# A decoder kernel with the gated decay attention reordered and the cross attention stepped, its scores split in three

## The chip, the cores and the metric

One Trainium2 chip, one core, one launch. The time is the device time of that core in microseconds (us). Profiles are of one execution each. Engines: TensorE (PE, its weight loads PEld), VectorE (DVE), ScalarE (ACT), GpSimd (POOL) and SyncE (SP), which starts the DMAs.

## The reference

A two-layer decoder with layer norm after every part, on x of 2 x 256 tokens of 512 features and a context of 2 x 512 tokens. Each part adds to x, and x is then normalised:

1. causal attention, 32 heads of 128 with 8 key heads, rotary embedding, some keys scaled by 1.5 or 0.5
2. a cross product of x and the context, both rounded to 8 bits
3. a mixing of four streams with a Sinkhorn normalisation of 50 rounds
4. gated decay attention ("l1" in the kernel): queries and keys with rotary embedding, products weighted by exp of summed decays, times values; each head's result is divided by its root mean square, multiplied by the gate, and projected out
5. cross attention ("x"): queries from x, keys and values from the context, both queries and keys divided by their root mean square, softmax over 512 keys, values, projection
6. a 512 x 512 linear map with LoRA parts

Parts 4 and 5 are what the change rewrites.

```
att = softmax(rms(q) . rms(k) / sqrt(128) + mask) @ v      # part 5, per head
x   = layernorm(x + att @ Wo)
y   = ((q . k) * exp(g_i - g_j) * dt_j) @ v                # part 4, per head, j <= i
z   = rms(y) * silu(gate)
x   = layernorm(x + z @ Wo)
```

## The kernel before

Each engine has its own instruction list, written by hand in Python; the order of the list is the order of execution, and semaphores (`wait_ge`, `then_inc`) join the lists. All of x stays in SBUF as four tiles of 128 tokens by 512. The 32 heads are worked in eight groups of four that share a key head; a loop body handles one group g, with buffers alternating by p = g % 2. `piped_groups` writes out the first two and last two groups and loops over the rest.

**Split products.** A matmul of fp32 operands is made of two parts: a high part rounded to fp32r and the rest, low = x - high. `product` (L175 to L181) issues three matmuls: high x high (L179), low x high (L180), high x low (L181). `project_split` does a projection of one head for all 512 tokens, `out_split` one output tile: 12 matmuls of 128 x 512 each, a block in what follows. Attention scores, values and transposes are plain fp32 matmuls, two records each in the profile.

**Decay attention** (`l1_tensor` and the functions beside it). TensorE, for one group: key projection into bank 0, values (32 short records, L1161), four queries, gates 0 and 1, scores(0) of the first sequence (3 matmuls, L1121), gates 2 and 3, outputs(0) (decay times value, L1134 and L1137), scores(1), transposes of z 0 and 1 (`turn_z`, L1145), output tile 0, outputs(1), output tile 1, transposes 2 and 3, output tiles 2 and 3. ScalarE copies projections for the rotary embedding (L148 to L150), takes exponentials and squares, and casts weights to their high part (L966). GpSimd does the sine product (L157), the low part of weights, the gate products and the power -1/2. VectorE does the rotary sum (L163, L167), the decay exponents (L1325), clamps gates (`clamp`), weights scores, makes z (`gated`, L1361), takes the low part of z (`rest`, L1369) and adds tiles to x (L215). All z tiles are transposed in bank 2, one behind the other: `turn_z` of tile n waits for the low part of tile n - 1.

**Cross attention** (`x_tensor` and the functions beside it). A group has eight steps, one for each head and sequence, head outermost. Step s: scores (two matmuls of 128 x 512, L1573, to banks 3 and 4), scale and mask into `logit` (L1814), maximum (L1818), exponentials on ScalarE (L1688), normalise on VectorE (L1826), transposes of probabilities (L1584), their copy (L1697), values (L1596), and the attention as high part (ScalarE, L1706) and low part (VectorE, L1835). TensorE runs scores(s), turn_probs(s-2), values(s-3). VectorE runs logits(s) ahead of normalise(s-1). The four queries of the next group are projected in between, two in the first steps and two in the last; key transposes and all four output tiles come behind the last step. GpSimd makes both parts of wq and wo (`split`: L187 high, L191 low).

**First attention** (`l0_tensor`). It has the form that the cross attention gets: in each of eight steps TensorE issues scores(s), turn_probs(s-1), one block, values(s-1), the block being a query or an output tile of the group before, this one or the next.

SyncE's list starts each weight load once the buffer's reader of the group before has signalled; `l1_wq`, `l1_wg` and `l1_wo` have one buffer each, the cross attention's have two.

## Time and profile before

| | us |
|---|---|
| median of 3 runs | 1659.37 (1658.19 to 1660.63) |
| the profiled execution | 1658.7 |
| its span, first to last instruction | 1656.7 |
| TensorE busy | 1484.6 (90%) |
| VectorE busy | 1075.8 (65%) |
| ScalarE busy | 788.2 (48%) |
| GpSimd busy | 659.9 (40%) |

The execution runs through its stages in order: the first attention up to about 375, cross product, mixing and the context's keys and values up to about 541, the decay attention up to about 1062, the cross attention up to about 1613, the linear map to the end. "Busy" of TensorE counts modelled ends that overlap, so it overstates how much of it is used at its peak; start-to-start distances tell what it really takes. PEclk is the clock granted to TensorE as a share of its full 2.4 GHz.

### The profile page before, as it was taken

How to read it: one execution, taken by the hardware profiler on the slowest of the kernel's cores; microseconds unless marked ns; L12 is line 12 of the kernel's file. 1: busy time of each engine (PE TensorE's matmuls, PEld its weight loads, DVE VectorE, ACT ScalarE, POOL GpSimd, SP SyncE). 2: the span in 40 equal slices, each digit the busy share in tenths (PEclk: the TensorE clock that was granted, in tenths of full speed). 3: DMA queues.
4: the chain of work that ended last, by engine and by line, in shares of the span. 5: the costliest groups of instructions: out<-in, count | busy, mean ns of one | idle time of the engine just before them, and what ended most of it. 6: DMA issues, size and time to landing. Idle time of an engine off the chain costs nothing.

```text
span 1656.7 us, 23145 instructions
## 1 busy us (share of the span) xinstructions
PE 1484.6 (90%) x7186; PEld 1161.1 (70%) x7186; DVE 1075.8 (65%) x2399; ACT 788.2 (48%) x2014; POOL 659.9 (40%) x671
## 2 busy tenths in 40 slices
PE   6999999987999589889889889789898898999996
PEld 5778888774988367767767767567676686776672
DVE  4696776876788676566566566545847648457462
ACT  4655666551222355555465465344545336345340
POOL 4544554420222346446456445363515415333200
PEclk9999999999999699999999999789999999999998
DMA  7011111003132222212212211410120210201000
GB/s 285 1 64 64 64 63 63 30 1 139 42 113 100 96 72 90 89 51 90 89 51 89 89 51 36 155 39 14 64 76 1 76 40 37 76 13 56 1 1 25
DMA packets 30120, 107.56 MB, mean 65 GB/s; under 512 B 3847, under 2 KB 13191, under 8 KB 22104
## 3 DMA queue, kind: packets, MB, share of 16 engines
q1 hardware_dynamic: 30040, 106.58, 17.7%
q8 instruction: 39, 0.64, 0.2%
q14 instruction: 41, 0.34, 0.1%
HBM read 97.07 MB, written 9.50 MB: 64 GB/s over the span
## 4 chain that ended last, share of the span: by engine, by line
PE 49%; issue 20%; DVE 19%; ACT 5%; POOL 5%; DMA 1%; POOLq 0%; DVEq 0%; ACTq 0%; SPq 0%
PE bank L179 9%; PE bank L180 8%; PE bank L181 8%; PE bank L1596 4%; PE bank L1573 3%; DVE logit L1814 2%; PE bank L1584 2%; DVE prob L1826 2%; POOL tmp L157 2%; PE bank L1134 2%; PE bank L278 1%; DVE tmp L1792 1%; PE bank L309 1%; PE bank L1121 1%; PE bank L1542 1%
## 5 line engine op out<-in xcount | busy, mean ns | idle before, releaser
L157 POOL TENSOR_TENSOR tmp<-tmp,sin 128x512 f32<-128x512 f32 x80 | 121.3, 1517 | 209.3 <-ACT tmp L150 208.9
L1688 ACT ACTIVATE prob<-logit,rmax 128x512 f32<-128x512 f32 x128 | 91.3, 715 | 153.8 <-DVE rmax L1818 153.8
L181 PE MATMUL bank<-wo_low,att_high 128*128 128x512 f32 x384 | 155.4, 405 | 0.0
L1573 PE MATMUL bank<-kT,qT 128*128 128x512 f32 x256 | 123.6, 606 | 10.6 <-DVE logit L1814 9.5
L179 PE MATMUL bank<-l_wo_high,att_high 128*128 128x512 f32 x256 | 111.6, 436 | 10.6 <-DVE att_low L558 10.6
L1596 PE MATMUL bank<-probT,v 128*128 128x256 f32 x512 | 121.1, 379 | 0.0
L1814 DVE SCALAR_TENSOR_TENSOR logit<-bank,qss,amask 128x512 f32<-128x512 f32 x128 | 92.4, 743 | 34.5 <-PE bank L1573 25.1
L1457 PE MATMUL bank<-kT,wg 128*128 128x256 f32 x512 | 110.9, 379 | 0.7 <-ACT prob L1475 0.7
L1457 PEld LDWEIGHTS bank<-kT,wg 128*128 128x128 f32 x512 | 97.1, 190 | 14.2 <-ACT prob L1475 1.1
L215 DVE TENSOR_TENSOR x<-x,bank 128x512 f32<-128x512 f32 x96 | 64.8, 683 | 64.3 <-PE bank L181 63.6
L180 PE MATMUL bank<-l_wo_high,att_low 128*128 128x512 f32 x256 | 105.3, 411 | 0.0
L180 PE MATMUL bank<-xT_high,wq_low 128*128 128x512 f32 x256 | 103.4, 404 | 0.0
L163 DVE TENSOR_TENSOR tmp<-tmp,cos 128x512 f32<-128x512 f32 x80 | 75.5, 944 | 41.9 <-ACT tmp L150 41.9
L1596 PEld LDWEIGHTS bank<-probT,v 128*128 128x128 f32 x512 | 92.8, 190 | 10.6
L1584 PEld LDWEIGHTS bank<-ident,prob 128*128 128x128 f32 x512 | 57.7, 140 | 57.2 <-DVE prob L1826 46.0
L1750 POOL TENSOR_TENSOR qss<-qss,half 128x4 f32<-128x4 f32 x32 | 33.8, 1064 | 143.9 <-DVE qss L1797 143.9
L148 ACT ACTIVATE tmp<-bank 128x512 f32<-128x512 f32 x80 | 47.4, 593 | 90.0 <-PE bank L181 83.3
L1697 ACT ACTIVATE probT<-bank 128x512 f32<-128x512 f32 x128 | 69.6, 598 | 42.6 <-PE bank L1584 42.3
L181 PEld LDWEIGHTS bank<-wo_low,att_high 128*128 128x128 f32 x384 | 75.4, 196 | 18.2
L1584 PE MATMUL bank<-ident,prob 128*128 128x128 f32 x512 | 67.7, 275 | 22.5 <-DVE prob L1826 22.3
L167 DVE TENSOR_TENSOR qT<-tmp 128x512 f32<-128x512 f32 x64 | 62.1, 970 | 32.7 <-POOL tmp L157 31.4
L1826 DVE TENSOR_SCALAR prob<-prob,rsum 128x512 f32<-128x512 f32 x128 | 81.5, 678 | 2.3
(254 smaller groups left out, 4017.3 us busy)
## 6 DMA issues: line engine op xcount, KB each, us to landing
wq<-in_l_wq SPq DMA_DIRECT2D x16, 1024.0 KB, 5.9
wo<-in_l_wo SPq DMA_DIRECT2D x16, 1024.0 KB, 4.8
wkv<-in_l_wkv SPq DMA_DIRECT2D x16, 512.0 KB, 5.6
wg<-in_l_wg SPq DMA_DIRECT2D x8, 1024.0 KB, 4.7
wq<-in_x_wq SPq DMA_DIRECT2D x8, 1024.0 KB, 7.0
wo<-in_x_wo SPq DMA_DIRECT2D x8, 1024.0 KB, 4.8
kT<-in_x_wkv SPq DMA_DIRECT2D x8, 512.0 KB, 4.1
kv_keys<-logit SPq DMA_DIRECT2D x8, 512.0 KB, 4.6
```

The source lines that it names most:

```text
L157: eng.tensor_tensor(halves(tmp[4 + j % 2]), halves(tmp[2 + j % 2]), per_batch(sin), ALU.mult).then_inc(sem(f"{l}_sinp"), 1)
L163: eng.tensor_tensor(halves(tmp[j % 2]), halves(tmp[j % 2]), per_batch(cos), ALU.mult).then_inc(sem(f"{l}_cosp"), 1)
L179: eng.matmul(dst, a_high, b_high, start=start, stop=False)
L180: eng.matmul(dst, a_low, b_high, start=False, stop=False)
L181: return eng.matmul(dst, a_high, b_low, start=False, stop=stop)
L1457: last = pe.matmul(bank[KV_BANKS[n % 2]][:, i * 256:(i + 1) * 256], wg[t // CT][:, c, t % CT * P:(t % CT + 1) * P], weights[:, c, :], star ...
L1573: pe.matmul(bank[3 + c][:, :], qT[p][:, h, b * L + c * P:b * L + (c + 1) * P], kT[p][:, b * C:(b + 1) * C], start=True, stop=True)\
L1584: last = pe.transpose(bank[5 + half_][:, kt * L + c * P:kt * L + (c + 1) * P], prob[s % 2][:, c, (2 * half_ + kt) * P:(2 * half_ + kt + 1) ...
L1596: last = pe.matmul(bank[VALUE_BANKS[s % 2]][:, 0:L], v[p][:, b * CT + kt, :], probT[s % 2][:, kt, :], start=(kt == 0), stop=(kt == CT - 1))
L1688: last = act.activation(prob[s % 2][:, c, :], logit[s % 2][:, c, :], ACT.Exp, bias=rmax[s % 2][:, c:c + 1], accum_out=rsum[s % 2][:, c:c + 1])
L1814: dve.scalar_tensor_tensor(logit[s % 2][:, c, :], bank[3 + c][:, :], qss[p][:, 1, h, 2 * b + c:2 * b + c + 1], amask[:, c, :], ALU.mult, A ...
L1826: last = dve.tensor_scalar(prob[s % 2][:, c, :], prob[s % 2][:, c, :], rsum[s % 2][:, 2 + c:3 + c], None, ALU.mult)
```

## The change

Decay attention: `l1_scalar`, `l1_gpsimd`, `l1_vector` are reordered to match a new order of TensorE. Its body is now (the order before is told above):

```
+                query(0)
+                query(1)
+                if isinstance(g, int) and g == 0:
+                    dt_turn(pe)
+                query(2)
+                query(3)
+                gates(0)
+                gates(1)
                 scores(0)
                 gates(2)
+                outputs(0, 0)
+                outputs(0, 1)
+                scores(1)
                 gates(3)
+                if not last_group:
+                    key(n)
+                    value(n, 1 - p, (0, 1))
+                outputs(1, 0)
                 turn_z(0)
+                outputs(1, 1)
                 turn_z(1)
                 out_tile(0)
                 out_tile(1)
                 turn_z(2)
                 turn_z(3)
+                if not last_group:
+                    value(n, 1 - p, (2, 3))
                 out_tile(2)
                 out_tile(3)
```

n is g + 1. The next group's key goes to bank 0 once `gates(3)` has been clamped; its values go to bank 1. z tiles are transposed to banks 2 and 5 by turns; output tiles go to banks 3, 4, 0 and 6 (before 1, 0, 3, 4). VectorE's order behind the ropes is now:

```
                 clamp(0)
                 clamp(1)
                 weights(0)
                 clamp(2)
-                clamp(3)
                 low_weights(...)                           # wo
+                weights(1)
                 mean(0)
+                clamp(3)
+                gated(0)
                 mean(1)
-                gated(0)
                 gated(1)
                 rest(0)
-                weights(1)
+                mean(2)
                 rest(1)
-                mean(2)
+                rope_sum(dve, "l1", n, 0, kT[1 - p][:, 0:T])
+                gated(2)
                 mean(3)
-                gated(2)
                 gated(3)
                 rest(2)
                 rest(3)
```

ScalarE takes both `decays` ahead of the sigmoids, the casts of wo and wq between sigmoids 0, 1 and 2, and squares(2) ahead of headed(1); GpSimd makes wq's low part and two powers ahead of gates 2 and 3. For the first group, ScalarE copies the key and the value ahead of the transposed decay columns (`cols`, which waits for `dt_turn`).

Cross attention: steps run sequence outermost, and TensorE's body is

```
+                for s in range(STEPS):
+                    scores(s)
+                    if s or not first:
+                        turn_probs(s - 1)
+                    if s < 2:
+                        query(g, p, s + 2, ...)
+                    elif s < 4:
+                        if not first:
+                            out_late(s)                    # tiles 2, 3 of group g - 1
+                    elif s < 6:
+                        if not last_group:
+                            query(n, 1 - p, s - 4, ...)
+                    else:
+                        out_early(s - 6)                   # tiles 0, 1 of group g
+                        if not last_group:
+                            turn_keys(n, 1 - p, s - 6, ...)
+                    if s in (1, 2):
+                        query_sums(g, s + 1)
+                    if s in (5, 6) and not last_group:
+                        query_sums(n, s - 5)
+                    if s or not first:
+                        values(s - 1)
```

with split scores in place of one fp32 matmul per bank, for which queries and keys get low parts on VectorE:

```
-                        pe.matmul(bank[3 + c][:, :], qT[...], kT[...], start=True, stop=True)
+                        product(pe, bank[3 + c][:, :], (q_high[p][:, h, rows_], q_low[p][h][:, rows_]),
+                                (k_high[p][:, keys_], k_low[p][:, keys_]), True, True)
+            def keys_rest(m, p, half_):
+                dve.scalar_tensor_tensor(k_low[p][at], bank[5 + half_][:, :], dvec[:, 3:4],
+                                         k_high[p][at].bitcast(F32), ALU.mult, ALU.subtract)
+            def query_rest(m, p, h):
+                dve.tensor_tensor(q_low[p][h][:, :], bank[h % 2][:, :], q_high[p][:, h, :].bitcast(F32),
+                                  ALU.subtract)
```

VectorE's step is, with each condition and its call on one line,

```
+                for s in range(STEPS):
+                    logits(s)
+                    if s >= 2 or not first: low(s - 2)
+                    if s == 0 and not first: add(g - 1, 1)
+                    if s in (1, 2): query_rest(g, p, s + 1)
+                    if s in (3, 4) and not first: add(g - 1, s - 1)
+                    if s == 4 and not last_group: x_key_mean(dve, n)
+                    if s in (5, 6) and not last_group: query_rest(n, 1 - p, s - 5)
+                    if s == 7 and not last_group: add(g, 0)
+                    normalise(s)
+                    if s in (1, 2): query_mean(g, p, s + 1)
+                    if s in (5, 6) and not last_group: query_mean(n, 1 - p, s - 5)
+                    if s == 5 and not last_group: norm_keys(n, 1 - p)
+                    if s in (6, 7) and not last_group: keys_rest(n, 1 - p, s - 6)
```

ScalarE's step is turned(s-1), exps(s), then weight casts (steps 4 and 5: wo in 3 + 1 chunks; 6 and 7: wq of group g + 2, two chunks each), a query (steps 0, 1, 4, 5), squares of the next keys (2, 3), keys_out (6, 7), headed(s-1). GpSimd only takes the low parts of the weights, chunk by chunk, and the powers. In the last group all four adds and the statistics of the layer norm come behind low(7). The squares, mean and power of the first keys move ahead of the layer norm between the stages, and the mask is loaded ahead of the keys. In the first attention only a semaphore is renamed. One buffer (`klow0`, 128 x 1024) is added.

## Rows read from the trace of the kernel before

**Rows 1.** Windows: from:to, length, busy of PE PEld DVE ACT POOL, PEclk, DMA share, GB/s
```profile
135.00:260.00 125.00, 121.53 (x690) 103.10 (x688) 86.01 (x196) 79.21 (x202) 60.08 (x61) 1.00 0.16 64
729.50:790.90 61.40, 54.59 (x266) 43.10 (x265) 38.40 (x89) 33.73 (x83) 32.60 (x30) 0.97 0.23 78
790.90:852.20 61.30, 54.53 (x265) 43.00 (x265) 38.05 (x88) 33.68 (x83) 33.05 (x30) 0.97 0.22 77
795.90:803.00 7.10, 5.44 (x20) 4.32 (x21) 5.53 (x18) 1.38 (x2) 0.00 (x0) 0.76 0.01 3
1262.80:1329.70 66.90, 62.46 (x299) 46.81 (x297) 41.78 (x68) 30.84 (x82) 25.14 (x21) 1.00 0.13 48
1329.70:1396.60 66.90, 62.46 (x299) 46.81 (x297) 41.80 (x68) 30.84 (x82) 25.14 (x21) 1.00 0.13 48
```

**Rows 2.** Waits of TensorE in one decay group: total us, times, longest
```profile
PE bank L1145 <- DVE att_low L1369: 3.1, 2, 1.6
PE bank L1145 <- issue: 2.5, 1, 2.5
```

**Rows 3.** Waits of TensorE in one cross attention group
```profile
PE bank L1584 <- DVE prob L1826: 2.9, 2, 1.7
```

**Rows 4.** Timeline of TensorE in a decay group: start, duration, records
```profile
798.59 0.66 PE L179 MATMUL bank<-l_wo_high,att_high 128*128 128x512 f32 x1
...
799.91 0.63 PE L179 MATMUL bank<-l_wo_high,att_high 128*128 128x512 f32 x1
...
849.33 1.28 PE L1134 MATMUL bank<-v,probT 128*128 128x128 f32 x10
850.45 0.39 PE L1137 MATMUL bank<-v,tmp 128*128 128x128 f32 x2
```

**Rows 5.** Timeline of TensorE in a cross attention group
```profile
1193.59 1.88 PE L1573 MATMUL bank<-kT,qT 128*128 128x512 f32 x4
1195.30 1.04 PE L1584 MATMUL bank<-ident,prob 128*128 128x128 f32 x8
1196.18 1.89 PE L1596 MATMUL bank<-probT,v 128*128 128x256 f32 x8
1197.90 1.88 PE L1573 MATMUL bank<-kT,qT 128*128 128x512 f32 x4
...
1202.46 0.40 PE L180 MATMUL bank<-xT_high,wq_low 128*128 128x512 f32 x1
1202.69 0.40 PE L181 MATMUL bank<-xT_low,wq_high 128*128 128x512 f32 x1
```

**Rows 6.** Groups by line: busy us, mean ns, idle before
```profile
L1814 DVE SCALAR_TENSOR_TENSOR logit<-bank,qss,amask 128x512 f32<-128x512 f32 x128 | 92.4, 743 | 34.5 <-PE bank L1573 25.1 <-ACT prob L1688 7.7
...
L1818 DVE TENSOR_REDUCE rmax<-logit 128x2 f32<-128x1024 f32 x64 | 78.1, 1220 | 2.2
...
L1688 ACT ACTIVATE prob<-logit,rmax 128x512 f32<-128x512 f32 x128 | 91.3, 715 | 153.8 <-DVE rmax L1818 153.8
...
L966 ACT ACTIVATE l_wo_high<-wo 128x512 fp32r<-128x512 f32 x32 | 17.6, 620 | 0.2
```

**Rows 7.** The normalise line alone: ns min/median/max
```profile
L1826 DVE TENSOR_SCALAR prob<-prob,rsum x128: 473/487/1494, 1104.7 to 1595.9; 128x512 f32<-128x512 f32 x128
```

**Rows 8.** Timeline where the two stages begin and end
```profile
594.19 2.74 PE L1121 MATMUL bank<-qT,kT 128*128 128x512 f32 x6
...
1062.26 0.69 DVE L215 TENSOR_TENSOR x<-x,bank 128x512 f32<-128x512 f32 x1 [1.03 <-PE bank L181]
...
1071.60 0.80 PE L179 MATMUL bank<-xT_high,wq_high 128*128 128x512 f32 x1 [1.41 <-DVE xT_low L661]
...
1093.23 3.75 PE L1573 MATMUL bank<-kT,qT 128*128 128x512 f32 x4 [1.01 <-ACT kT L1673]
...
1613.08 0.69 DVE L215 TENSOR_TENSOR x<-x,bank 128x512 f32<-128x512 f32 x1 [1.50 <-PE bank L181]
```

**Rows 9.** Timeline of VectorE: the gated products of two tiles
```profile
807.15 2.34 DVE L1361 SCALAR_TENSOR_TENSOR q<-bank,yss,q 128x128 f32<-128x128 f32 x8
```

More of the change, by code:

```diff
@@ L1729, in x_scalar @@
+                if last_group:
+                    turned(7)
+                    headed(7)
             query(0, 0, 0)
-            squares(0, 0)
-            for h in range(1, GH):
-                query(0, 0, h)
-            keys_out(0, 0)
+            query(0, 0, 1)
+            for half_ in range(2):
+                keys_out(0, 0, half_)
             piped_groups(nc.scalar, body)
@@ L1852, in body, with add @@
[L1852 to L1864 removed]
+                def add(m, t):
+                    residual_add(dve, "x", m, t, bank[t % 2])
```

716 lines of the change are left out of this document (392 added, 324 removed).

## The prediction

> **What bounds the kernel now.** The windows come first: in the two attention stages that the change rewrites, TensorE is the busiest engine by far, 54.5 of 61.3 us of a group of the gated decay stage and 62.5 of 66.9 us of a group of the cross attention, with VectorE second (38 and 42 us) [rows 1]. Both stages repeat a group eight times with a fixed period: neighbouring stretches of 61.4 and 61.3 us of the decay stage hold the same work (266 and 265 matmul records), and so do two of 66.9 us of the cross attention (299 each), so these are the periods [rows 1]. The waits of TensorE come next. In the decay stage it waits 5.6 us of a group in front of the transposes of z (L1145), the longest 2.5 us [rows 2]; in the cross stage 2.9 us in front of the transposes of the probabilities, the longest 1.7 [rows 3]. So the price of both is mostly TensorE's own work plus some ends of a dependent chain. A third thing shows in the clock: between 795.9 and 803.0 the granted clock is 0.76 [rows 1], right behind the longest wait, and there the products of two heads start 1.32 us apart (798.59 to 799.91) [rows 4], where three matmuls at full clock take 0.70 (below).
>
> **Floors by counting TensorE's work.** Start-to-start times are used, since modelled ends overlap. A split product streams one matmul each 0.2325 us (1202.46 to 1202.69 [rows 5]), so a block of 12 is 2.79 us. An fp32 matmul of 512 columns is two records 0.43 us apart: four records of L1573 go from 1193.59 to 1195.30, 1.72 us [rows 5].
> Decay stage, one group: 13 blocks of 12 (key, 4 queries, 4 gates, 4 outputs) 36.3; 12 score records at 0.43, 5.2; 96 short records (32 of the values, 48 of decay times value, 16 transposes) at 0.112 (ten in 1.12 us, 849.33 to 850.45 [rows 4]), 10.8. Sum 52.3 us, against 61.3.
> Cross stage, one group: 8 blocks of 12, 22.3; scores 8 x 1.72 = 13.8; transposes of probabilities 8 x 0.88 = 7.0 (1195.30 to 1196.18); values 8 x 1.72 = 13.8 (1196.18 to 1197.90); 32 short records of the sums of squares and 8 key transposes at 0.11, 4.4 [rows 4, 5]. Sum 61.3 us, against 66.9.
> The first attention already has the stepped form that the cross attention gets, and in a stretch of it TensorE is busy 121.5 of 125.0 us at clock 1.00 [rows 1]: the form can be run with 3% lost.
>
> **Cross attention, scores.** Each score product goes from one fp32 matmul to three split ones: 6 x 0.2325 = 1.40 in place of 1.72 us a step, 2.6 us less a group. That is only TensorE. VectorE gets four query remainders and two key remainders a group, all 128x512 from a bank, nearest to L1814 at 0.74 [rows 6]: 4.4 us, bringing it from 41.8 to 46 of 60. ScalarE gets eight casts of weights, 0.62 us each (L966 [rows 6]), 5 us, on its 30.8 [rows 1]; GpSimd loses as many. Neither is near its limit. A split stream that starts behind short transposes loses a further 0.1 us, an estimate, some five times more often than before: 0.5 us. Floor of the new group: 61.3 - 2.6 + 0.5 = 59.2.
> Is the step chain covered? VectorE now does normalise(s) ahead of logits(s+1), so its chain is serial: logits and maximum 2 x 0.70 + 1.22, two exponentials 2 x 0.72 with an accumulator read, 1.6, normalise 2 x 0.49 [rows 7] with its reciprocal, 1.1, and hops of 0.2: 5.5 us a step [rows 6]. A TensorE step is scores 1.4, transposes 0.9, a block 2.8, values 1.7, in some sums 0.8: 6.8 to 8.1, mean 7.4. The chain is covered by 1.3 us or more. Where it is thin: step 5 puts the key norms behind normalise (1.3 to 3.4 us), and keys must be turned, cast and subtracted by ScalarE and VectorE in step 6, before the first half of the next transposes; by my count it arrives 0.2 us early. I take 0.8 us of waits a group, 60.0. The bounds are 59.2 (none) and 63.5 (step 5 to 7 all late).
> The normalise row shows what can eat the cover: median 487 ns, but up to 1494 [rows 7], the long ones where GpSimd runs a split; at the long end a normalise adds 2 us and uses the cover up. The Trainium skill (GPSIMD Engine Reference, 8. Key points) has a rule for it: GpSimd contends with VectorE instructions that have two SBUF inputs or run in a 2-port mode. By that rule the remainders read from a bank are free of it, and the six rope sums and gated products of a decay group are not; no row here prices the difference.
> Ends of the stage: the first group starts its scores 10.5 us after the first query instead of 21.6 (1093.23 less 1071.60 [rows 8]), because two queries are left to steps 0 and 1: 4.6 for the first query at the slow clock, 2.8, key transposes 0.9, two casts 1.4, a remainder 0.7. Steps of the first group: 4.2 (nothing to turn), 9.9 (the transposes wait 2.2 for the first normalise), 4.8 and 4.4 (no output block of a group before), 7.6, 7.6, 8.1, 7.2: 54 us. Groups 1 to 6 take 6 x 60. The last group has no next queries in steps 4 and 5, which the chain binds (5 and 6), and ends with output tiles 2 and 3 (9.5): 6.8 + 7.6 + 7.6 + 6.8 + 5 + 6 + 6.5 + 6.8 + 9.5 = 62.6. Sum 10.5 + 54 + 360 + 62.6 = 487. Before, from 1071.60 to the last residual add at 1613.08: 541.5. Gain 54.4 us. Against it, at the end four adds and four statistics now stand behind the last remainder on VectorE, +1.6 us; and a key mean on VectorE and its power on GpSimd (about 1.6 us) stand in front of the layer norm between the stages, +1.2 us. Net 51.6.
>
> **Decay stage.** Nothing is computed differently; the key and value of group g+1 move among the gates and outputs of g, outputs and z alternate, banks are spread. TensorE's 52.3 us stand. The count from the end of gates(3): the next key uses the same bank, so it waits for clamp(3), 0.9 us. VectorE goes on with gated(0), 1.1 (half of the eight products of L1361 [rows 9]), GpSimd's power 1.0, gated(1) 1.1: 4.9 us after gates(3). Then it waits for the headed copies of tiles 0 and 1, which follow TensorE's transposes (rests until 10.9), makes the key's rope sum (12.4), gated(2) (13.5), power, and gated(3): z(3) is ready at 15.9. TensorE has by then done the key 2.8, values 1.8, outputs 2.7, two transposes 0.9, two output tiles 5.6 and one transpose 0.4 behind its wait of 0.9: 15.1, so 0.8 us of wait. In front of scores(0) the last rope sum is done 15.8 us into the group and TensorE arrives at 16.7. So 54 us if all goes as counted; I add 1 us for VectorE slowed by GpSimd: 55, bounds 52.3 and 58. The slow-clock stretch goes with the long wait.
> Entry costs: query(0) now needs the value bank copied out by ScalarE, which comes behind the decay setup; and the transposed columns are copied only after query(1). In times of the trace: value copied by 574.6, query(0) 4.6 at the slow clock, query(1) 2.8, columns copied by 583.4, two queries' copies 3.6, then queries (2) and (3) and two gates to 596.2, where scores(0) start; now they start at 594.19 [rows 8]. In a settled group they start 16.7 us in, so the first starts in effect at 579.5. The last group lacks the next key and value, 6.3 us. End: 579.5 + 8 x 55 - 6.3 = 1013.2 against 1062.0, just ahead of the last residual add at 1062.26 [rows 8]. Gain 48.8 us.
> The earlier mask load and the weight loads (1 MB in 5 to 7 us) lie beside work; the semaphore rename in the first attention costs nothing.
>
> **Sum.** 48.8 + 51.6 = 100.4; the profiled span 1656.7 becomes 1556.3, and its own time 1658.7 becomes 1558.3. That execution lies 0.7 us under the median of the runs, so 1559.
>
> **Rivals.**
> (a) All waits go: 52.3 and 59.2 a group. Decay gains 8 x 2.7 = 22 more, cross 6: 1531. For it, the first attention's 3%; against it, the clamp that the key waits for can't vanish.
> (b) The decay stage keeps half of its waits: VectorE's chain with GpSimd's power in it (gated, mean, power, gated) slips 2 to 3 us a group, period 58: +24, 1583. For it, VectorE is full of short dependent pieces there. The clock is a price on top: waits of up to 1.7 us in a cross group left it at 1.00 [rows 1, 3], and the 2.5 us wait was followed by 0.76 [rows 1, 2]; were the short ones to cost as that one did, (803.0 - 795.9) x 0.24 = 1.7 us a group, it would be 14 us in the stage, within this case. The Trainium skill (TensorE: Matmul & The Clock Gate, A second HAM failure mode: psum-queue depth-cycling) says that frequent short idles between groups of matmuls can swing the clock; by that rule the 14 us would be owed, the trace does not agree in the cross attention.
> (c) The cross steps are bound by the chain: keys late in step 6 and normalise at 1.5 us each, 3 to 4 us a group: 63.5 in place of 60, +28: 1587. (b) and (c) together: 1611.
> (d) Slower than before: ScalarE's moved work closes the chain. Casts (up to three, 1.9 us) and a query's copy and square (1.2) stand on its queue between the exponentials of one step and the next transposed copies (1.2) and attention copy (0.4); if TensorE's order made each step wait for all of them, a step is 5.5 + 4.7 = 10.2 us, 82 a group, 8 x 22 = +176: 1735. It decides from 9.1 us a step (66.9 / 8 = 8.4, and 48.8 / 64 = 0.8 for what the decay stage gives). Against it: only steps 4 to 7 carry casts, and TensorE's block of 2.8 us lies over them.
> (e) The split scores don't stream at 0.2325 because each score product is a chain of only three: at 0.43 each they would cost 2.6 a step, +76 us: 1635. Against: the same shapes stream in the blocks, and behind a block change only 0.1 us is lost.
>
> **How the numbers follow.** Forecast 0.50, (a) 0.13, (b) 0.17, (c) 0.11, both 0.04, (e) 0.02, (d) 0.03. The range 1530 to 1600 takes in (a), (b) and (c). The measurement tells 0.2% (3 us). Faster 0.96, same 0.01, slower 0.03.
>
> **What would show it.** The period of L1121 near 55 and of the scores near 60; granted clock 1.00 in a decay group; TensorE's waits: one near 0.9 behind the clamp in front of the key, one near 1 in front of L1145's successor; split scores 0.23 us apart; scores(0) of the first decay group near 596; VectorE near 46 of 60 us. I am wrong if a period exceeds 58 or 63, or if the products' spacing differs.

## The result, and the profile after

The changed kernel takes 1553.28 us (median of 4 runs, 1549.13 to 1555.81) against 1660.00 (4 runs, 1658.19 to 1661.41): a ratio of 0.9354, 95% interval 0.9343 to 0.9365. The forecast was 1559, range 1530 to 1600. The profiled execution took 1555.24 us, its span is 1553.3, at a mean granted clock of 0.973.

The page's line of busy times, and then windows of the changed kernel: the stretch of the first attention, two neighbouring periods of a decay group, two of a cross attention group (columns as in [rows 1]).

```profile
PE 1439.7 (93%) x7314; PEld 1179.8 (76%) x7314; DVE 1080.7 (70%) x2447; ACT 823.0 (53%) x2074; POOL 587.0 (38%) x611
```

```profile
135.00:260.00 125.00, 120.93 (x686) 102.53 (x684) 86.60 (x197) 79.68 (x204) 60.19 (x60) 1.00 0.16 63
709.80:764.60 54.80, 52.51 (x264) 42.02 (x264) 38.52 (x88) 33.61 (x82) 31.97 (x30) 1.00 0.25 87
764.60:819.40 54.80, 52.53 (x264) 42.01 (x264) 38.63 (x88) 33.62 (x82) 31.88 (x30) 1.00 0.25 87
1099.00:1157.70 58.70, 58.70 (x314) 50.19 (x313) 40.98 (x73) 35.60 (x91) 16.28 (x13) 1.00 0.15 55
1157.70:1216.40 58.70, 58.70 (x313) 50.10 (x313) 41.26 (x73) 35.53 (x90) 16.26 (x13) 1.00 0.15 54
```

Against [rows 1]: a decay group takes 54.8 us instead of 61.3, with the same work of VectorE (38.5) and ScalarE (33.6); a cross group 58.7 instead of 66.9, and in it TensorE has no gap at all, busy 58.70 of 58.70. ScalarE has taken on the casts (35.6, before 30.8), GpSimd has given them up (16.3, before 25.1). VectorE has 41, not the 46 that was forecast. The six remainders are there (4.2 us), but its normalisations take 8.1 us a group instead of 10.9 and its two products of the keys 1.3 instead of 3.4, since fewer long operations of GpSimd lie beside them. With the casts back on GpSimd (an experiment below) the normalisations take 9.1 and the products of the keys stay at 1.3, so most of this comes from where the operations now fall, and only about 1 us from the casts.

Of the 6.5 us of a decay group, about 4.4 are waits of TensorE (6.7 in all before, 2.3 now) and about 1.7 are its clock: the stretch at 0.76 that each group had behind its longest wait [rows 1] is gone, and the group's mean goes from 0.97 to 1.00.

What is left of TensorE's waits, first in the one decay group from 709.8 to 764.6, then in the whole cross attention from 1040 to 1500 (total us, times, longest). In the window of one settled cross group there is no wait to list.

```profile
PE bank L180 <- DVE q L1380: 1.8, 1, 1.8
PE bank L1173 <- DVE q L1405: 0.3, 1, 0.3
PE bank L1149 <- DVE qT L168: 0.2, 1, 0.2
```

```profile
PE bank L1653 <- DVE prob L1939: 2.9, 3, 1.4
PE bank L1611 <- DVE q_low L1907: 2.2, 1, 2.2
PE bank L1667 <- ACT probT L1773: 1.2, 3, 0.4
```

The 5.6 us in front of the transposes of z [rows 2] have become 0.3 (L1173). A wait of 1.8 stands in front of the key (L180), behind the clamp of the last gates (L1380); the kernel before had a shorter one of this kind, in front of its third gates, in seven of the eight groups:

```profile
PE bank L179 <- DVE q L1336: 0.9, 1, 0.9
```

The 2.9 us of each cross group [rows 3] have become 2.9 us in the whole stage, all in its first and last group. A second wait of the kernel before, 1.3 us a group in front of the scores for VectorE's logits, which the prediction did not name, is gone too.

The place of the key's wait, on TensorE and on VectorE (timelines: start, duration):

```profile
723.07 0.40 PE L182 MATMUL bank<-l_wg_low,xT_high 128*128 128x512 f32 x1
725.22 0.48 PE L180 MATMUL bank<-xT_high,l_wk 128*128 128x512 f32 x1 [1.75 <-DVE q L1380]
```

```profile
716.77 4.05 DVE L974 TENSOR_TENSOR wo_low<-wo,l_wo_high 128x512 fp32r<-128x512 f32 x3
720.74 2.15 DVE L1389 SCALAR_TENSOR_TENSOR probT<-bank,gc,probT 128x128 f32<-128x128 f32 x8
722.81 1.11 DVE L1389 SCALAR_TENSOR_TENSOR tmp<-bank,gc,tmp 128x128 f32<-128x128 f32 x4
723.84 0.64 DVE L1396 TENSOR_SCALAR yss<-yss 128x4 f32<-128x4 f32 x1
724.39 0.68 DVE L1380 TENSOR_SCALAR q<-bank 128x512 f32<-128x512 f32 x1
```

Gates 3 are finished at about 723.5, but VectorE comes to the clamp only at 724.39: the low part of the output weights and the twelve products of `weights(1)` stand ahead of it.

The values of one cross step, the split scores of the next, two products of three matmuls, and the transposes behind them:

```profile
1186.44 1.89 PE L1667 MATMUL bank<-probT,v 128*128 128x256 f32 x8
1187.98 0.58 PE L180 MATMUL bank<-k_high,q_high 128*128 128x512 f32 x1
1188.40 0.39 PE L181 MATMUL bank<-k_high,q_low 128*128 128x512 f32 x1
1188.62 0.40 PE L182 MATMUL bank<-k_low,q_high 128*128 128x512 f32 x1
...
1189.56 1.03 PE L1653 MATMUL bank<-ident,prob 128*128 128x128 f32 x8
```

The scores take 1189.56 - 1187.98 = 1.58 us, against 1.71 of the four fp32 records [rows 5]; but their first record starts 1.54 behind the values, where an fp32 one started 1.72 behind them (1196.18 to 1197.90 [rows 5]), and its successor 0.19 later than the stream. Values and scores together are 3.12 instead of 3.44 or so.

The edges: the first queries of the decay stage, their window, its first scores, and the first query and first scores of the cross attention.

```profile
576.39 0.77 PE L180 MATMUL bank<-xT_high,l_wq_high 128*128 128x512 f32 x1 [3.27 <-ACT v L1228]
...
587.78 0.51 PE L180 MATMUL bank<-xT_high,l_wq_high 128*128 128x512 f32 x1 [2.22 <-ACT tmp L151]
...
600.54 1.88 PE L1149 MATMUL bank<-qT,kT 128*128 128x512 f32 x4
...
1027.39 0.49 PE L180 MATMUL bank<-xT_high,wq_high 128*128 128x512 f32 x1 [1.41 <-DVE xT_low L662]
...
1036.03 0.72 PE L180 MATMUL bank<-k_high,q_high 128*128 128x512 f32 x1
```

```profile
576.20:582.10 5.90, 5.71 (x14) 4.48 (x15) 0.84 (x2) 0.05 (x1) 1.28 (x1) 0.50 0.89 320
```

The entry of the decay stage is one of two places where the change costs something (the other is the layer norm between the stages, below): behind the wait of 3.27 us the granted clock is 0.50, so the 1.2 GHz level, for 5.9 us. The second wait, of 2.2, is not new (the kernel before has it at 576.99), but behind it, too, TensorE runs at 0.50 from 589.1 to 592.1.

The first group of the cross attention has two more stretches at half clock:

```profile
1036.10:1039.40 3.30, 3.30 (x9) 2.62 (x9) 1.64 (x5) 0.00 (x0) 1.99 (x2) 0.50 0.24 88
1057.80:1060.10 2.30, 2.30 (x7) 1.83 (x6) 0.37 (x1) 0.38 (x1) 2.15 (x2) 0.52 0.00 0
```

Where the profiled 103.4 us came from (1656.7 less 1553.3), by the last residual additions of the two stages, which are at 1016.78 and 1510.20 now:

```profile
1016.78 0.69 DVE L216 TENSOR_TENSOR x<-x,bank 128x512 f32<-128x512 f32 x1 [1.43 <-PE bank L182]
...
1510.20 0.67 DVE L216 TENSOR_TENSOR x<-x,bank 128x512 f32<-128x512 f32 x1
```

Up to the last addition of the decay stage 45.5 (1062.26 [rows 8] less 1016.78); from there to the first cross query -1.3 (9.34 before, 10.61 now); the cross attention from its first query to its last addition 58.7 (541.5 before, 482.8 now); behind it 0.5. This execution was not one of the shortest: the part behind the last addition takes 43.1 us here at a mean clock of 0.82, and 41.1 at 0.86 in the kernel with three moves at the edges (below), which has the same instructions there.

### The profile page after: what moved, and what is told of

It is laid out like the page before. It is cut to its first block, busy times and chain, and to the rows that moved or that the text cites. A ratio compares the mean times of both kernels' runs of the same rounds, so it can differ in the third digit from the quotient of the medians.

```text
span 1553.3 us, 23538 instructions
## 1 busy us (share of the span) xinstructions
PE 1439.7 (93%) x7314; PEld 1179.8 (76%) x7314; DVE 1080.7 (70%) x2447; ACT 823.0 (53%) x2074; POOL 587.0 (38%) x611
## 3 DMA queue, kind: packets, MB, share of 16 engines
q1 hardware_dynamic: 30040, 106.58, 18.9%
## 4 chain that ended last, share of the span: by engine, by line
PE 56%; issue 17%; DVE 15%; POOL 8%; ACT 3%; DMA 1%; POOLq 0%; SPq 0%; DVEq 0%; ACTq 0%
PE bank L180 11%; PE bank L181 11%; PE bank L182 11%; PE bank L1667 7%; PE bank L1653 3%; PE bank L1611 2%; PE bank L1149 2%; PE bank L279 1%; POOL yss L1330 1%; PE bank L310 1%; POOL tmp L158 1%; DVE tmp L164 1%; POOL q L1323 1%; PE bank L333 1%; DVE q L686 1%
## 5 line engine op out<-in xcount | busy, mean ns | idle before, releaser
L158 POOL TENSOR_TENSOR tmp<-tmp,sin 128x512 f32<-128x512 f32 x80 | 115.4, 1443 | 232.2 <-ACT tmp L151 229.2
L182 PE MATMUL bank<-wo_low,att_high 128*128 128x512 f32 x384 | 150.6, 392 | 0.0
L1667 PE MATMUL bank<-probT,v 128*128 128x256 f32 x512 | 124.4, 386 | 1.2 <-ACT probT L1773 1.2
L180 PE MATMUL bank<-l_wo_high,att_high 128*128 128x512 f32 x256 | 104.7, 409 | 11.8 <-DVE att_low L559 10.6
L149 ACT ACTIVATE tmp<-bank 128x512 f32<-128x512 f32 x80 | 47.6, 595 | 113.5 <-PE bank L182 110.4
L181 PE MATMUL bank<-l_wo_high,att_low 128*128 128x512 f32 x256 | 99.8, 390 | 0.0
L182 PEld LDWEIGHTS bank<-wo_low,att_high 128*128 128x128 f32 x384 | 72.0, 188 | 16.8
L417 ACT ACTIVATE prob<-logit,rmax 128x128 f32<-128x128 f32 (+1 forms) x128 | 57.3, 448 | 48.9 <-DVE rmax L541 48.2
L1931 DVE TENSOR_REDUCE rmax<-logit 128x2 f32<-128x1024 f32 x64 | 78.1, 1220 | 2.2
L537 DVE TENSOR_TENSOR logit<-bank,keys 128x384 f32<-128x384 f32 x64 | 35.4, 552 | 51.3 <-PE bank L312 50.7
```

The lines of the kernel that those rows point to most:

```text
L158: eng.tensor_tensor(halves(tmp[4 + j % 2]), halves(tmp[2 + j % 2]), per_batch(sin), ALU.mult).then_inc(sem(f"{l}_sinp"), 1)
L180: eng.matmul(dst, a_high, b_high, start=start, stop=False)
L181: eng.matmul(dst, a_low, b_high, start=False, stop=False)
L182: return eng.matmul(dst, a_high, b_low, start=False, stop=stop)
L1667: last = pe.matmul(bank[VALUE_BANKS[s % 2]][:, 0:L], v[at][:, b * CT + kt, :], probT[s % 2][:, kt, :], start=(kt == 0), stop=(kt == CT - 1))
L1931: dve.tensor_reduce(rmax[s % 2][:, 0:2], logit[s % 2][:, :, :], AX.X, ALU.max, negate=True)\
```

## The experiments

Each edit is against the changed kernel unless it says otherwise. A kernel's line numbers shift by a few where lines were added. "Slower" and "faster" are against its 1553.28 us; the kernel before lay at 1659.4 to 1660.3 in each set.

### The decay part alone

The kernel before, with the functions of the decay attention as changed.

> The kernel before with the decay attention's part of the change alone. Theory (the two stages gain on their own, each by the waits that left TensorE's list): the scores of two decay groups are 54.8 us apart instead of 61.3, seven times, and the last group is some 3 us shorter, so 45 to 52 us are gained and the time is near 1612. Rival 1 (the change of the cross attention is what gains, and the decay part's waits are only pushed to another place): under 25 us gained, over 1635. Rival 2 (the two parts help each other, because the cross attention's first group starts on what the last decay group prepares): under 40 us gained here and in the counterpart together with this less than the whole 107.

Measured 1612.43 us (1611.06 to 1616.59), ratio to before 0.9709, interval 0.9695 to 0.9724: 47.8 us gained. TensorE's waits in its decay stage are those of the changed kernel, seven times the key's wait among them:

```profile
PE bank L179 <- DVE q L1379: 12.5, 7, 2.3
```

### The cross part alone

The changed kernel, with the functions of the decay attention as before.

> The kernel after with the decay attention's part as it was before: the cross attention's steps, split scores and split keys alone. Theory: groups of 58.7 us instead of 66.9, seven times (57 us), and a start of the scores that is some 12 us earlier after the first query, less 3 us of tail and layer norm: 56 to 66 us gained, 1595 to 1604. Rival 1 (the decay part carries the gain): under 30 us, over 1630. Rival 2 (the parts help each other): this and its counterpart together fall short of the whole 107 us by more than 5.

Measured 1597.66 us (1596.45 to 1599.78), ratio 0.9627, interval 0.9612 to 0.9641: 62.6 us gained. Its decay stage has the old waits in front of the transposes of z:

```profile
PE bank L1146 <- DVE att_low L1370: 22.3, 14, 1.7
PE bank L1146 <- issue: 17.5, 7, 2.5
```

47.8 + 62.6 = 110.4, and both together gave 106.7. The parts are independent within what the runs can tell, and each has the gain that its theory said; rivals 1 and 2 fall. The 3.7 us are no more than the intervals of the three ratios allow.

### Scores as one fp32 product

```
-                        product(pe, bank[3 + c][:, :], (q_high[p][:, h, rows_], q_low[p][h][:, rows_]),
-                                (k_high[p][:, keys_], k_low[p][:, keys_]), True, True)
+                        pe.matmul(bank[3 + c][:, :], qT[p][:, h, rows_], kT[p][:, keys_],
+                                  start=True, stop=True)
```

> The kernel after with the cross attention's scores as one fp32 product of TensorE instead of three products of fp32r parts; the remainders of queries and keys are still computed and not used. Theory: TensorE is without waits in this stage and so each microsecond of it counts: the two fp32 products of a step took 0.43 us for each of 2 records, 1.72 in all, the six split ones are 0.2325 apart, 1.40, so 0.32 a step, 64 steps, about 20 us slower, near 1574. Rival 1 (the steps' chain over VectorE and ScalarE bounds the stage): 0 to 5 us. Rival 2 (split products don't stream, or the split costs what it saves): 0, or faster than the kernel after.

Measured 1572.16 us (1571.24 to 1575.54), ratio 0.9475, interval 0.9461 to 0.9490: 18.9 us slower. Its window of one group:

```profile
1154.02:1215.33 61.31, 61.31 (x298) 47.20 (x297) 41.68 (x73) 35.57 (x92) 16.16 (x13) 1.00 0.15 52
```

61.31 less 58.7 is 2.6 us a group, 0.33 a step, and TensorE is full in both. So of the cross attention's 62.6 us the split gave 19. The other 44 are what remains: the order of the steps, the edges and the casts moved to ScalarE (7 us by an experiment below) together, with no run for the order alone. And a microsecond taken from TensorE's list here is a microsecond of the kernel.

### Values ahead of the key

```
                 if not last_group:
-                    key(n)
                     value(n, 1 - p, (0, 1))
+                    key(n)
```

> The kernel after with the first half of the next decay group's values ahead of its key, so that TensorE has 1.9 us of work while VectorE clamps the last gates. Theory: the key's wait on the clamp (11.9 us in seven groups) goes, and nothing is late next: 8 to 12 us faster, 1541 to 1545. Rival (the values wait on the same VectorE, whose clamp of the tile before is also late, or what is moved later, the key's copies and its rotation, delays the next group): 0 to 4 us.

Measured 1539.41 us (1539.36 to 1541.07), ratio 0.9277, interval 0.9264 to 0.9289: 13.9 us faster. The first scores of two neighbouring groups are now 53.08 us apart:

```profile
704.61 2.84 PE L1149 MATMUL bank<-qT,kT 128*128 128x512 f32 x6 [0.20 <-DVE qT L168]
...
757.69 2.84 PE L1149 MATMUL bank<-qT,kT 128*128 128x512 f32 x6 [0.27 <-DVE qT L168]
```

The key's wait (11.9 us in seven groups) is gone from the list and took most of the 0.3 us of L1173 with it (2.3 us in seven groups became 0.6 in four). From the first to the last group's scores it is 370.2 us instead of 382.6, so 12.4. Theory confirmed: nothing was late next, and the 1.9 us beyond its upper end are within the spread of the runs.

### 1.2 us more in the chain of each cross step

```
+                    for host in ((0, 1), (2, 3))[s % 2]:
+                        act.activation(spare[host][:, :], logit[s % 2][:, 0, :], ACT.Copy)
                     for c in range(2):
                         last = act.activation(prob[s % 2][:, c, :], ...
```

> The kernel after with two more copies of 128x512 on ScalarE ahead of the exponentials of each of the 64 cross steps (their output is used by nothing): about 1.2 us more in the chain from the scores to the normalised probabilities, and 9.5 us more of ScalarE in a group (35.6 of 58.7 us before). Theory (the chain has cover: a step of TensorE is 6.8 to 8.1 us, the chain 5.5 and the next transposes come 1.3 us or more after it): 0 to 3 us slower, only in the last group, whose steps have little beside them. Rival (the chain, not TensorE, sets the step, and TensorE only looks full): 64 times 1.2, 77 us slower.

Measured 1564.90 us (1563.37 to 1568.53), ratio 0.9433, interval 0.9421 to 0.9446: 11.6 us slower. Neither side was right: the chain doesn't set the step (77 would have shown), yet something of it reaches TensorE in each group, for the settled groups are 59.9 us long, 1.2 more. In a settled group of the changed kernel the chain's cover, the time by which the last normalisation ends before TensorE starts the transposes, is 1.2 to 3.3 us (1205.37 - 1202.11 at the most, 1153.85 - 1152.61 at the least), so plain 1.2 us should cost nothing. One view of VectorE and GpSimd tells where. First the changed kernel at step 4 of a group, then this one, whose step is 1.2 later relative to the weights:

```profile
1186.76 0.88 DVE L1939 TENSOR_SCALAR prob<-prob,rsum 128x512 f32<-128x512 f32 x2
```

```profile
1186.06 1.64 POOL L1843 TENSOR_TENSOR kss<-kss,half 128x8 f32<-128x8 f32 x1 [11.72 <-DVE kss L1887]
1187.66 3.78 POOL L1581 TENSOR_TENSOR wo_low<-wo,wo_high 128x512 fp32r<-128x512 f32 x3
```

```profile
1192.34 1.94 DVE L1944 TENSOR_SCALAR prob<-prob,rsum 128x512 f32<-128x512 f32 x2
```

```profile
1192.70 3.98 POOL L1584 TENSOR_TENSOR wo_low<-wo,wo_high 128x512 fp32r<-128x512 f32 x3 [0.47 <-ACT wo_high L1581]
```

```profile
1194.34 1.09 PE L1656 MATMUL bank<-ident,prob 128*128 128x128 f32 x8
...
1203.58 0.48 PE L180 MATMUL bank<-wo_high,att_high 128*128 128x512 f32 x1 [0.48 <-POOL wo_low L1584]
```

In the changed kernel the normalisation ended at 1187.64, 0.02 us ahead of GpSimd's weights, which stood behind the power of the key sums. In this one they wait for ScalarE's cast, start between the two normalisations, and the pair takes 1.94 instead of 0.88. So 1.2 us of chain became 2.3 at that step, and TensorE starts at 1194.34, when it ends; a second wait, 0.48, stands later behind GpSimd. The starts of TensorE's records, laid beside those of the changed kernel, tell what each costs in a settled group. In front of the transposes it is 0.25 us: their cover was 1.9 (1187.64 to 1189.56), enough for 1.2 and not for 2.3. In front of the output tile that waits for GpSimd's fourth chunk it is 0.73: the tile starts 1.52 behind the transposes (1202.06 to 1203.58), and 0.79 behind them in the changed kernel (1197.24 to 1198.03). In front of the transposes where the cover was 1.2 it is 0.1.

Six settled groups are 1.15 us longer each, 6.9 in all. The first group is 2.7 us longer (60.3 instead of 57.6) and the last one 2.4 (66.7 instead of 64.3); in them some steps have no block to lie over the chain, and TensorE waits 3.8 and 4.0 us for it instead of 0.2 and 2.7. That is 12.0 for the stage in the profiled executions, against 11.6 in the medians.

The Trainium skill (SBUF — State Buffer, SBUF: two separate sides) says that a VectorE operation in a 2-port mode and a GpSimd operation lock each other out of a shared pair of ports for the whole instruction; by that rule the second normalisation waits for one GpSimd operation, 3.98 / 3 = 1.3 us, an estimate, and the trace agrees in size (1.06 us longer). It does not agree for every operation of GpSimd: the power of the key sums (1.64 us from 1186.06) was under way when the changed kernel's two normalisations began at 1186.76, and they took 0.88 all the same. The trace doesn't show in which mode a normalisation runs.

### 2.4 us more in the chain

As the one before, and on VectorE:

```
+                    dve.tensor_reduce(rmax[s % 2][:, 4:6], logit[s % 2][:, :, :], AX.X, ALU.max, negate=True)
                     dve.tensor_reduce(rmax[s % 2][:, 0:2], logit[s % 2][:, :, :], AX.X, ALU.max, negate=True)
```

> As the one with two more copies on ScalarE a step, and one more maximum over 128x1024 on VectorE ahead of the real one (1.2 us): 2.4 us more in each step's chain. Neither engine is full by it (VectorE 50.8, ScalarE 45 of 58.7 us). Theory: the cover of the shortest steps, 1.3 us by the prediction, is used up, and what is over shows as TensorE's wait before the transposes of the probabilities: about 1.1 us in the four shorter steps of each group and less in the others, 8 groups, 20 to 50 us slower. Rival 1 (the cover is larger than the prediction says): under 10 us. Rival 2 (the chain sets the step): 150 us.

Measured 1624.98 us (1623.65 to 1628.70), ratio 0.9797, interval 0.9783 to 0.9810: 71.7 us slower, far over the theory's 20 to 50 and under half of rival 2. The group is 67.5 us long, 8.7 more than in the changed kernel, with VectorE busy only 50.5:

```profile
1167.85:1235.37 67.52, 60.77 (x313) 49.63 (x312) 50.49 (x83) 43.40 (x107) 16.46 (x13) 1.00 0.14 48
```

VectorE's timeline shows a closed ring: reciprocal to reciprocal it waits for ScalarE, and in some steps for GpSimd.

```profile
1179.47 0.17 DVE L1942 RECIPROCAL rsum<-rsum 128x2 f32<-128x2 f32 x1 [1.78 <-ACT prob L1769]
...
1186.87 0.17 DVE L1942 RECIPROCAL rsum<-rsum 128x2 f32<-128x2 f32 x1 [1.70 <-ACT prob L1769]
...
1189.23 1.41 DVE L1932 SCALAR_TENSOR_TENSOR logit<-bank,qss,amask 128x512 f32<-128x512 f32 x2 [1.21 <-POOL qss L1854]
...
1195.65 0.17 DVE L1942 RECIPROCAL rsum<-rsum 128x2 f32<-128x2 f32 x1 [1.70 <-ACT prob L1769]
```

A plain step of the ring takes 7.40 us (1179.47 to 1186.87), so 5.0 without the 2.4 that were added; a step in which the next head's mean goes to GpSimd for its power takes 8.78, so 6.4. The expectation had counted the plain chain alone (5.5) and a wait of 1.1 in the four shorter steps. But in the steps with a power the ring is 1.4 us longer, and a step that ends late makes the next one start late. TensorE's waits show both: 35.7 us in the stage for the normalised probabilities, and 19.3 in front of the sums of squares, for the query remainders that VectorE makes ahead of its late normalisation.

### Weight casts on GpSimd again

```
-            act.activation(high[:, c, :], t[:, c, :], ACT.Copy).then_inc(sem(done), 1)
+            pool.tensor_tensor(high[:, c, :], t[:, c, :], ones[:, 0:1].broadcast_to([P, t.shape[2]]),
+                               ALU.mult).then_inc(sem(done), 1)
```

with the waits for the loads moved along.

> The kernel after with the high parts of the cross attention's weights computed on GpSimd again (8 more operations of some 1.25 us a group there, 8 copies of 0.61 less on ScalarE). Theory (both engines have room; the move was needed for nothing while the chain has cover): within 3 us of the kernel after. Rival 1 (GpSimd's operations lengthen VectorE's beside them and the remainders come later, so that the queries of the next group wait): 5 to 25 us slower. Rival 2 (ScalarE's casts stand in the chain): faster by 3 us or more.

Measured 1560.49 us (1558.59 to 1567.03), ratio 0.9421, interval 0.9404 to 0.9438: 7.2 us slower, rival 1. The wait is not in the queries, which it named, but in the output tiles, 1.2 us on average in seven groups, and a settled group is 60.2 us long, 1.5 more:

```profile
PE bank L180 <- POOL wo_low L1582: 8.6, 7, 1.3
```

### One bank for the transposes of z

```
-        Z_BANKS = [2, 5]
+        Z_BANKS = [2, 2]
-                    pe.wait_ge(sem("att_low"), L1_ATT + 4 * g + m - 1)
+                    pe.wait_ge(sem("att_low"), L1_ATT + 4 * g + m)
```

> The kernel after with one bank of PSUM for the transposes of the decay group's gated outputs instead of two, so that each transpose waits until both parts of the one before have been read. Theory (the second bank is one of the edits that took waits off TensorE): the transposes of tile 3 come right behind those of tile 2 and wait for a copy on ScalarE (0.7) and a remainder on VectorE (0.7), 1.3 to 1.7 us in 8 groups, and little for tile 1: 8 to 16 us slower. Rival (ScalarE and VectorE are behind at this place anyway, and the wait only moves): 0 to 4 us.

Measured 1561.06 us (1559.58 to 1562.57), ratio 0.9405, interval 0.9392 to 0.9417: 7.8 us slower, at the lower edge of the theory. The wait is as expected, 1.6 us a group; 0.3 of it the same instruction waited for its z before, and a group is 56.10 us long (first scores at 713.56 and 769.66), 1.3 more:

```profile
PE bank L1173 <- DVE att_low L1413: 11.2, 7, 1.7
```

### Three moves at the edges

```
-            value(0, 0)                          # ScalarE, behind the key's copies; now ahead of the rows' exponentials
-                query(1)
                 if isinstance(g, int) and g == 0:
                     dt_turn(pe)
+                query(1)
+            x_key_pow(pool, 0)                   # behind ln_gpsimd(pool, 3) instead of ahead of it
```

> The kernel after with three small moves at the edges of the stages: ScalarE copies the first decay group's values ahead of the exponentials of the rows and of the key's copies, TensorE turns the rows between the first and the second query instead of after the second, and GpSimd raises the layer norm's power ahead of the keys' power. Theory: the waits of 3.3 and 2.2 us at the entry of the decay stage go, the queries that ran at half the clock behind the first of them (13 records some 0.43 apart instead of 0.23) run at full clock, and the layer norm starts 1.1 us earlier: 6 to 10 us faster, near 1545. Rival (the rows' vector chain or ScalarE's later copies are late next): 1 to 4 us.

Measured 1543.33 us (1542.87 to 1547.86), ratio 0.9308, interval 0.9294 to 0.9322: 10.0 us faster. The key and the queries run on without a gap, at full clock:

```profile
574.58 0.80 PE L1007 MATMUL bank<-ident,qT 32*128 32x32 f32 x10
575.31 0.50 PE L180 MATMUL bank<-xT_high,l_wq_high 128*128 128x512 f32 x1
...
591.72 2.84 PE L1152 MATMUL bank<-qT,kT 128*128 128x512 f32 x6 [0.63 <-DVE qT L168]
```

The first scores start at 591.72 instead of 600.54; 1.3 us of the 8.8 are the earlier start of the stage in this run. A wait of 1.4 us remains, now in front of the first gates. The layer norm between the stages, from the last addition to the first cross query, takes 9.3 us instead of 10.6.

### The fourth chunk of output weights earlier, with 1.2 us more in the chain

Against the kernel with two more copies a step:

```
-                    if s == 4:
-                        out_weights((0, 1, 2))
-                    if s == 5:
-                        out_weights((3,))
+                    if s == 4:
+                        out_weights((0, 1, 2, 3))
```

and on GpSimd the fourth chunk ahead of `query_pow(g + 1, 1 - p, 0)`.

> The kernel with two more copies on ScalarE a cross step (alone 1564.9 us, 11.6 slower than the kernel after, its groups 1.16 us longer), and in it the fourth chunk of the output weights is split together with the first three, on ScalarE in step 4 instead of 5 and on GpSimd ahead of the power of the next query. Theory (the chain reaches TensorE by a side way: that power waits for VectorE's step, and the fourth chunk stands behind it in GpSimd's queue; TensorE waits 0.48 for it in each group): 3 to 5 us faster than that kernel, near 1561, and the rest of its loss stays, since it is the normalisation of one step that now runs beside GpSimd's weights (1.94 instead of 0.88 us). Rival (the wait for the weights only covers a wait for the chain itself): 0 to 1 us.

Measured 1561.44 us (1559.90 to 1561.79), ratio 0.9402, interval 0.9389 to 0.9415, against 0.9433 (0.9421 to 0.9446): 3.5 us faster than its counterpart. The wait for `wo_low` is gone from the list, and a settled group takes 59.2 us instead of 59.9. So 0.7 of the 1.2 us a settled group was a side way: the power waits for VectorE's mean, which stands behind the step's normalisation, and the fourth chunk stood behind the power.

### All four moves, and the statistics

The three moves at the edges and the values ahead of the key:

> The three moves at the edges together with the values ahead of the decay group's key (alone 13.9 us faster than the kernel after). Theory: they touch different waits and add up, 20 to 24 us faster than the kernel after, 1529 to 1533. Rival (one gives the other's gain back): 14 to 18 us.

Measured 1530.24 us (1529.10 to 1531.82), ratio 0.9219, interval 0.9207 to 0.9232: 23.0 us faster, where the two alone gave 13.9 and 10.0. They add up. With the statistics of each tile right behind its own addition as well:

> The four moves, and the layer norm's statistics of each tile right behind its addition instead of behind the next tile's. Theory: the statistics of the last tile but one no longer stand between the last addition and the last statistics: 0.6 us at each of five ends of a stage, 2 to 3 us faster than the kernel with the four moves. Rival (the wait of VectorE for its own addition, added four times, costs as much): 0 to 1 us either way.

Measured 1529.45 us (1528.30 to 1531.98), ratio 0.9214, interval 0.9201 to 0.9226: 0.8 us, not told apart from nothing; the rival. At the end of the cross attention the additions come back to back, VectorE is not idle between them, and the order of eight operations doesn't change when the last one ends.

The best version measured is thus at 1530 us, 7.8% under the kernel before and 1.5% under the changed one.

## Why the prediction was right, and where it was off

The mechanism is the one forecast: TensorE's waits went, nothing took their place in a settled cross group, and the two floors counted from start-to-start times hold (52.3 and 59.2 forecast; 52.5, the period less its waits, in a decay group, and 58.7 in a cross group). The clock of the decay groups came back with the longest wait, as forecast (0.97 to 1.00). By its terms:

- **Decay period, 55 forecast, 54.8 measured.** The total is right, its parts less so. The key's wait was put at 0.9 us and is 1.8; z(3)'s at 0.8 and is 0.3; 0.2 stands before the scores. The extra microsecond for a VectorE slowed beside GpSimd is what the key's wait holds: the low part of the output weights (three of its operations 4.05 us beside GpSimd, so 1.35 each, where the first, begun alone, took 0.7) and the products behind it delay the clamp. The prediction had named the rope sums and the gated products as what GpSimd would slow. The rope sums were slowed at times (0.69 to 1.67 us), but four gated products, which read a bank, took 1.13 beside GpSimd and 1.12 without it; the subtraction of the output weights and the decay exponents, which read two tiles of SBUF, were what grew most (four exponents 1.14 or 2.24). The swap of values and key showed that the key's wait was worth its whole length (13.9 us, of it 12.4 in the periods).
- **Cross period, 60 forecast, 58.7 measured: the largest error, 1.3 us in each of six groups, 7.8 in all.** Two terms of the sum were wrong: the allowance of 0.8 us for keys that come late in step 6, and the 0.5 us for the start behind short transposes. The first is not there: no wait in a settled group. Nor is the second: an fp32r matmul behind short fp32 ones delays its successor (0.42 and 0.31 us to the next start instead of 0.23), but starts earlier itself by as much, so the split saved its full 0.33 us a step, as the experiment with fp32 scores showed.
- **Ends of the cross attention.** First scores 8.6 us after the first query, 10.5 forecast: the queries ran at full clock, where the slow clock had been carried over from the kernel before. But the slow clock came right behind: the first group took 57.6 us (1036.03 to 1093.60), 54 forecast, with the two stretches at half clock shown above, some 1.7 us each. In five of the other kernels with the same steps it took 55.4 to 55.7, so about 2 of its 3.6 us are the clock of this run. The last one took 64.3, tail included, 62.6 + 1.6 forecast. Together with the periods 482.8 instead of 487 + 1.6.
- **Entry of the decay stage.** First scores forecast at 596.2; they came at 600.54 in a run whose stage began 1.9 us later, so 2.4 us were missed. The wait of 2.2 in front of query(2) is not the reason: from the turned columns to query(2) it was 3.0 us, as the sum implies (582.0 to 596.2 less four blocks of 2.79). What was missed is the clock. The first two queries took 8.4 us instead of 7.4, since the slow stretch lasted beyond the first of them, and a second slow stretch stood behind that wait, 1.6 us, which the sum did not have.
- **Layer norm between the stages.** +1.2 forecast, +1.3 measured.
- **The tail.** The four additions stand together behind the last remainder as forecast, and are inside the last group's 64.3.

Decay 45.5, its stage's later start of 1.9 included (48.8 forecast), cross less layer norm 57.4 (51.6 net forecast): two errors of opposite sign, -3 and +6, left 1555.2 instead of 1558.3 for the profiled execution. That they partly cancelled is luck. The median of the runs lies 2.0 us below that one.

The rivals. (a) Not all waits went, the key's stayed; the four moves together reach 1530, which is the time that rival gave. (b) Period 58: no. The granted clock stayed at 1.00 in the decay groups with waits of up to 1.8 us in each, as it had in the cross groups with 1.7 [rows 1, 3]. The rule of the Trainium skill that spoke for it (TensorE: Matmul & The Clock Gate, A second HAM failure mode: psum-queue depth-cycling) does not show in these groups; the 3.27 us wait at the entry was followed by 0.50. The length of a wait alone doesn't tell: one of 2.21 us in the first cross group was followed by half clock in the changed kernel (1057.8 to 1060.1) and by 1.00 in the kernel with three moves at the edges (1046 to 1056). (c) and (d) The chain doesn't bind; its cover in a settled group, 1.2 us at the least, is what the prediction counted (1.3). Yet the two kernels with a longer chain show that cover alone doesn't say what a longer chain costs. At 1.2 us more the kernel loses 11.6, at 2.4 more 71.7, and then the ring of VectorE, ScalarE and GpSimd sets most steps. The prediction missed three links of it: GpSimd's power in four of the eight steps (1.4 us), that the power and the fourth chunk of weights behind it carry a late step to TensorE (0.7 us a group), and that the three weight operations of GpSimd lie within 0.02 us behind a normalisation (0.25). (e) The scores stream at 0.23 us.

What stays open: no run took away the stretched normalisation alone, so its 0.25 us a settled group is read from the starts and not shown by an experiment; why a stretch at half clock comes in one run and not in another that has the same instructions there; and whether the 3.7 us between the sum of the parts and the whole are more than the spread of the runs.

## What to carry to other kernels

Count the busiest engine's list by start-to-start distances, stage by stage: that floor held within 1%, and what the change gained was the old waits plus the cheaper form of one product. Where a new wait stands behind another engine's queue, look for work in the waiting engine's own list that doesn't need it and put that first; this swap of two lines gave 14 us. A cover read as "step less chain" tells when the chain itself is late, not what hangs on it: add every engine that the ring passes through in any step, and look at what runs beside its links. Before you explain two microseconds at the edge of a stage by a wait, look at the granted clock there: here the clock, and not the wait, was what the forecast missed at the entry, and half of what it missed in the first cross group.

## What the runs showed of the hardware

- Two operations of VectorE from SBUF to SBUF, 0.88 us for the pair, took 1.94 when GpSimd's 128x512 subtraction had started ahead of the second one; beside GpSimd's power over 128x8 they kept their 0.88. The products that read a bank, beside the same subtractions, kept their length (two in 1.40 us). The changed kernel has one such long pair in each group (1.92 us at 1209.37).
- Three fp32r matmuls of 128x512 are 0.23 us apart also as a chain of three, but for the first behind fp32 ones, whose successor comes 0.42 later and which starts earlier by as much; one fp32 matmul of that shape is two records 0.43 apart. Six for four saved 0.33 us a step.
- The granted clock was 0.50 behind a wait of 3.27 us at the entry, and 1.00 throughout groups with a wait of 1.8. Behind a wait of 2.21 it was 0.50 in one kernel and 1.00 in another.
